# Moving the preparation items, the sums and the gate of a state-space loop by a step

## The reference

```python
xz = h @ in_proj_w.T;  x, z = split(xz, 2)
xc = silu(causal_conv4(x) + conv_b)
dt, Bm, Cm = split(xc @ x_proj_w.T);  dt = softplus(dt @ dt_proj_w.T + b)
deltaA = exp(dt[..., None] * A)                    # [B, L, 512, 16]
deltaBu = (dt * xc)[..., None] * Bm[:, :, None, :]
hst = deltaA_t * hst + deltaBu_t;  y_t = einsum('bdn,bn->bd', hst, C_t)
y = (y + D * xc) * silu(z);  out = y @ out_proj_w.T;  x = x + out
```

## Time and profile before

| | us |
|---|---|
| median of 3 runs (lowest, highest) | 2912.34 (2909.07, 2916.3) |
| the profiled execution's own time | 2912.34 |
| its span, first to last instruction | 2910.1 |
| mean granted TensorE clock | 0.89 |

### The profile page before, as it was taken

One profiled execution on the slowest core, in us unless ns is written; L12 is line 12 of the kernel. 1 busy time (PEld: TensorE's weight loads), 2 busy tenths in 40 slices (PEclk: granted clock), 3 DMA queues, 4 the chain that ended last, 5 costly groups with the idle time before them and its releaser, 6 DMA issues.

```text
span 2910.1 us, 38603 instructions
## 1 busy us (share of the span) xinstructions
PE 2412.2 (83%) x14260; PEld 1901.4 (65%) x14260; DVE 2051.3 (70%) x3042; ACT 1603.2 (55%) x2716; POOL 1052.1 (36%) x777
## 2 busy tenths in 40 slices
PE   5878787687998799858995678888777988899998
PEld 3555656566876588747883556565643443799998
DVE  6777768789997465538985767777955553567776
ACT  6665656344665455525884765656512445356663
POOL 2776767600000254210221667667811235100004
PEclk8989898889999799979997788898887787889999
DMA  4020212091000000022521220202056241246652
GB/s 150 1 95 13 83 43 76 28 358 50 23 1 1 35 1 30 12 68 91 181 82 47 94 88 8 95 1 95 12 85 108 47 103 59 86 149 218 218 207 91
DMA packets 98172, 235.14 MB, mean 81 GB/s; under 512 B 8901, under 2 KB 64977, under 8 KB 90818
## 3 DMA queue, kind: packets, MB, share of 16 engines
q1 hardware_dynamic: 85074, 209.85, 22.6%
q0 software_dynamic: 5376, 14.70, 1.5%
q10 hardware_dynamic: 7536, 8.13, 1.1%
HBM read 175.38 MB, written 48.81 MB: 77 GB/s over the span
## 4 chain that ended last, share of the span: by engine, by line
PE 51%; DVE 17%; ACT 15%; issue 7%; POOL 7%; DMA 1%; SPq 1%; POOLq 1%; ACTq 0%; DVEq 0%
PE psum L111 7%; PE psum L113 7%; PE psum L112 7%; PE psum L536 4%; PE psum L118 4%; PE psum L405 4%; PE psum L506 3%; POOL ch L430 3%; PE psum L519 2%; POOL bu L389 2%; ACT WH L3626 2%; ACT g L3773 2%; PE psum L482 2%; DVE ch L853 1%; PE psum L3067 1%
## 5 line engine op out<-in xcount | busy, mean ns | idle before, releaser
L389 POOL TENSOR_TENSOR bu<-u,row 128x1024 f32<-128x1024 f32 x158 | 371.8, 2361 | 219.8 <-DVE psum L853 132.1
L853 DVE TENSOR_TENSOR_SCAN psum<-psum,bu 128x1024 f32<-128x1024 f32 x128 | 292.7, 2287 | 94.8 <-ACT psum L663 94.8
L430 POOL TENSOR_TENSOR ch<-ch,row 128x1024 f32<-128x1024 f32 x128 | 300.8, 2355 | 149.2 <-DVE ch L853 149.2
L536 PE MATMUL psum<-ident,ch 128*128 128x128 f32 x2048 | 285.7, 288 | 69.0 <-POOL ch L430 68.3
L536 PEld LDWEIGHTS psum<-ident,ch 128*128 128x128 f32 x2048 | 247.3, 149 | 112.2 <-POOL ch L430 78.8
L853 DVE TENSOR_TENSOR_SCAN ch<-ad,psum 128x1024 f32<-128x1024 f32 x96 | 218.6, 2277 | 44.8 <-ACT ad L663 41.5
L405 PEld LDWEIGHTS psum<-row,uT 128*128 128x128 f32 x1536 | 202.7, 209 | 55.8 <-issue 36.8
L405 PE MATMUL psum<-row,uT 128*128 128x128 f32 x1536 | 208.6, 294 | 17.2 <-ACT uT L594 11.3
L663 ACT ACTIVATE psum<-dt,A 128x511 f32<-128x511 f32 x320 | 208.0, 683 | 0.3
L3773 ACT ACTIVATE g<-psum,bias 128x256 f32<-128x256 f32 x248 | 101.1, 470 | 133.8 <-PE psum L113 129.5
L875 DVE TENSOR_TENSOR ch<-psum,row 128x1024 f32<-128x1024 f32 x128 | 156.2, 1220 | 2.7
(11 more groups left out here) (469 smaller groups left out, 6954.2 us busy)
## 6 DMA issues: line engine op xcount, KB each, us to landing
W<-in_m1W SPq DMA_DIRECT2D x24, 2052.0 KB, 8.5
row<-Ascr SPq DMA_DIRECT2D x52, 512.0 KB, 4.9
row<-Bscr SPq DMA_DIRECT2D x52, 512.0 KB, 4.9
m1buf<-zt SPq DMA_DIRECT2D x8, 2048.0 KB, 16.7
W<-in_m0W SPq DMA_DIRECT2D x16, 1024.0 KB, 5.9
m1res<-ob ACTq DMA_DIRECT2D x23, 256.0 KB, 4.9
m0buf<-zt SPq DMA_DIRECT2D x2, 2064.0 KB, 17.6
xe<-m0buf SPq DMA_DIRECT2D x8, 516.0 KB, 8.1
```

Of the source, the lines that this page charges most:

```text
L389: e.tensor_tensor(m.bu[n % 2][:, :, :], u, m.row[:, g, 0, :, :], ALU.mult).then_inc(*m.fed.up)
L430: pool.tensor_tensor(o, o, m.row[:, i % UNITS, 1, :, :], ALU.mult).then_inc(*m.met.up)
L536: p = pe.matmul(m.y[:, c, :], m.ch[i % RING_C][:, j, 128 * c:128 * c + 128], k.ident, start=False, stop=g == UNITS - 1 and j == 1 and c == ...
L853: dve.tensor_tensor_scan(flat(to), flat(decays), flat(inputs), 0.0, ALU.mult, ALU.add).then_inc(*m.scan.up)
```

## The change

Three tables, two places in the order of a step, and some step numbers are changed; no computation is. On TensorE the sum of step i now follows the items of step i and the input of step i+2 (before, the input of step i+3 stood ahead of it). In `mamba_items` the items of the round before come first. The tables move most items by one step or two: z from 2-5 to 1-4, the three `yt` from 15, 19, 27 to 13, 18, 25, `out` from 7, 9, 11, 13 to 6, 8, 10, 12, `h` and `in` mostly one earlier, `conv` from 15, 16, 18, 20 to 15, 17, 19, 21, `xp` and `dt` one later. ScalarE does its part of a convolution one step after TensorE's. Its silu of z is at step 5, that of the convolution at 22, the exponentials of softplus at 26 and 27. VectorE's gate follows the first scan of the next group.

```diff
-OWN = {2: ("z", 0), 3: ("z", 1), 4: ("z", 2), 5: ("z", 3), 15: ("yt", 0), 19: ("yt", 1), 27: ("yt", 2)}
+OWN = {1: ("z", 0), 2: ("z", 1), 3: ("z", 2), 4: ("z", 3), 13: ("yt", 0), 18: ("yt", 1), 25: ("yt", 2)}
...
+    if b and s in BEFORE:
+        o.append((BEFORE[s][0], b - 1, BEFORE[s][1]))
     if s in OWN:
         o.append((OWN[s][0], b, OWN[s][1]))
...
     for i in range(PER * B):
+        s, g = i // UNITS, i % UNITS
+        for item in mamba_items(i):
+            mamba_item_pe(k, m, pe, *item)
         if i + 2 < PER * B and from_pe(i + 2):
             mamba_input_pe(k, m, pe, i + 2)
-        if i:
-            mamba_sum_pe(k, m, pe, i - 1)
-        for item in mamba_items(i):
-            mamba_item_pe(k, m, pe, *item)
-    mamba_sum_pe(k, m, pe, PER * B - 1)
+        if g == 0:
+            if s:
+                pe.wait_ge(*m.gated(s - 1))
+            pe.wait_ge(*m.dx_in(s))
...
+        pe.wait_ge(*mamba_out(m, i))
...
-        for item in mamba_items(i):
-            mamba_item_act(k, m, act, *item)
+        for item in mamba_items(i - 1) if i else []:
+            if item[0] == "conv":
+                mamba_item_act(k, m, act, *item)
+        for item in mamba_items(i):
+            if item[0] != "conv":
+                mamba_item_act(k, m, act, *item)
...
-        if n == 6:
+        if n == 5:
             mamba_gate_act(k, m, act, b)
...
-        if n == 21 and b + 1 < B:
+        if n == 22 and b + 1 < B:
             mamba_silu_act(k, m, act, b + 1)
-        if n in (25, 27) and b + 1 < B:
-            mamba_soft_exp_act(k, m, act, b + 1, n - 25, n - 23)
+        if n in (26, 27) and b + 1 < B:
+            mamba_soft_exp_act(k, m, act, b + 1, 2 * (n - 26), 2 * (n - 26) + 2)
...
-        if g == 1 and s:
+        if g == 0 and s:
             mamba_gate_dve(k, m, dve, s - 1)
```

More of the change, by code:

```diff
@@ L251 @@
 FIRST_BANKS = (0, 1, 2, 3, 4, 5, 6, 7, 0, 1, 3, 6, 2)
-OWN = {2: ("z", 0), 3: ("z", 1), 4: ("z", 2), 5: ("z", 3), 15: ("yt", 0), 19: ("yt", 1), 27: ("yt", 2)}
[L253 to L256, removed]
+OWN = {1: ("z", 0), 2: ("z", 1), 3: ("z", 2), 4: ("z", 3), 13: ("yt", 0), 18: ("yt", 1), 25: ("yt", 2)}
+BEFORE = {1: ("yt", 3), 6: ("out", 0), 8: ("out", 1), 10: ("out", 2), 12: ("out", 3)}
+AHEAD = {5: ("h", 0), 6: ("h", 1), 7: ("in", 0), 9: ("in", 1), 11: ("in", 2), 14: ("in", 3),
+         15: ("conv", 0), 17: ("conv", 1), 19: ("conv", 2), 21: ("conv", 3),
+         23: ("xp", 0), 24: ("dt", 0), 25: ("dt", 1), 26: ("dt", 2), 27: ("dt", 3), 30: ("bt", 0)}
 def mamba_items(i):
@@ L271, in mamba_items @@
         o.append((AHEAD[s][0], b + 1, AHEAD[s][1]))
-    if b and s in BEFORE:
-        o.append((BEFORE[s][0], b - 1, BEFORE[s][1]))
     return o
@@ L520, in mamba_item_pe @@
     p.then_inc(*m.full.up)
[L523 to L538, removed]
 def mamba_pe(k, m, pe):
@@ L545, in mamba_pe @@
     for i in range(PER * B):
+        s, g = i // UNITS, i % UNITS
+        for item in mamba_items(i):
+            mamba_item_pe(k, m, pe, *item)
         if i + 2 < PER * B and from_pe(i + 2):
             mamba_input_pe(k, m, pe, i + 2)
-        if i:
-            mamba_sum_pe(k, m, pe, i - 1)
-        for item in mamba_items(i):
-            mamba_item_pe(k, m, pe, *item)
-    mamba_sum_pe(k, m, pe, PER * B - 1)
+        if g == 0:
+            if s:
+                pe.wait_ge(*m.gated(s - 1))
+            pe.wait_ge(*m.dx_in(s))
+            for c in range(4):
+                p = pe.matmul(m.y[:, c, :], m.dx[:, 128 * c:128 * c + 128], k.ident, start=c == 0, stop=False, is_transpose=True)
+            p.then_inc(*m.direct.up)
+        pe.wait_ge(*mamba_out(m, i))
+        for j in range(2):
+            for c in range(4):
+                p = pe.matmul(m.y[:, c, :], m.ch[i % RING_C][:, j, 128 * c:128 * c + 128], k.ident, start=False,
+                              stop=g == UNITS - 1 and j == 1 and c == 3, is_transpose=True)
+        p.then_inc(*m.summed.up)
     mamba_item_pe(k, m, pe, "yt", B - 1, 3)
```

## The result

The changed kernel takes 2940.3 us (median of 4 runs, 2935.67 to 2942.08) against 2912.38 for the kernel before: ratio 1.0095, 95% interval 1.0077 to 1.0114. It is slower by 28 us. Forecast were 2900 us, faster by 12, with a range of 2870 to 2924: wrong in sign, and the time lies outside the range. The profiled execution took 2939.04 us, its span is 2936.8.

A forecast was written before the change was run, and what follows sets the result against it. VectorE's chain was taken as the frame, held by the order in TensorE's and ScalarE's queues. Rounds summed to −6.1 us a loop, −12.2 for two, from 2912.3 to 2900 us; range 2870 to 2924.

The forecast's parts named there:

- the start of a round: Up to scan 6 of a middle round: early gate and later inputs lose 4.7 us, bounds 0 and 6.
- the last round: Fourth round of a loop, nothing prepared for a next one: 3.7 us lost, with VectorE standing at step 24's gate.
- Steps 6 to 9: Output projection first in step 6: its large wait becomes three small ones, net loss 1.4 us including the start's.
- The wait of 9.89: VectorE's wait in us for the residual sum behind the output projection, which was held by ScalarE's silu and table load; forecast gone.
- The rival of the whole 9.89 gained: Larger gain: ScalarE catches up before step 6, 6.6 us more in four middle rounds, 2874 us; chance 0.18.
- Steps 9 to 32: Rest of a middle round: mainly an earlier x projection; step 25 is 4.1 us ahead, the round 130.9 instead of 136.3.
- the sign of a start 4 to 5 us earlier: Expected in the changed profile: the x projection starts that much earlier in the round, as u is copied before the silu.
- First round: First of a loop's four rounds: z projection ahead of the first input and later steps cost, the end gives back; 1 lost.
- Middle rounds: Second and third round of a loop: each lasts 130.9 us instead of 136.3, 5.4 saved.
- A loop: Four rounds of the state-space loop, run twice: +1.0 − 5.4 − 5.4 + 3.7 = −6.1 us.
- TensorE's lower clock as a term: At the start of a round, the sum the gate needs was taken at half clock, 1.97 us.
- The third one: Slower: gate one scan too early, its sum at half clock, 28 to 54 us, 2928 to 2954; chance 0.21.

The follow-up runs named there:

- the repeated run: The changed kernel, nothing edited, measured again on the chip of the two kernels with added zero-adding multiplications: 2937.29 us, 1.0072 of before.
- the filling: Changed kernel plus zero-adding multiplications in TensorE's idle time (9 before last sums, 3 before a round's first sum, 2 before its first z projection): 2915.94 us, 0.9996.
- 0.9913: The changed kernel with VectorE's gate back at step 1 and TensorE's old order, so new tables and late convolution copy remain: 2898.51 us.
- the mixed table: Kernel with late gate and old TensorE order, old step numbers up to 14, new from 15, items of the round before first: 2927.46 us, 1.0038.

## Why the prediction was wrong

**The step that failed.** The prediction put 4.7 us on the start of a round and priced the z projection and the input that now stand behind the first gate at full clock. Up to the scan of step 6 the start lost 5.8, 8.2 and 8.6 us in the second, third and last round. With the idle time filled, so that these multiplications do run at full clock, it lost 3.5 to 3.6 in all three. The second failed term is the last round, put at 3.7 lost and measured at 10.3.

**Start of the round: the gate right, what stands behind it too small.** 3.1 us were taken for the gate and 3.00 measured. But with 0.3 us lost, step 2 was to take 2.5 us to the next scan, and it took 4.08 in the second round and 6.66 in the third. In the third the z projection took 3.78 and the input 2.77; in the second both ran at full clock (1.98 and 1.95), and in the repeated run the z projection took 3.78 in both.

**Steps 6 to 9: right in kind.** The wait of 9.89 turned into smaller ones, 2.47 and 5.34 in the second round, where these steps took 3.1 us more than forecast. In the third the gate waited 2.57, as the 2.6 that I took, and they took 0.4 more. The rival of the whole 9.89 gained fell: ScalarE was in arrears.

**Steps 9 to 32: right, but from a later start.** From the first scan of the round, the scan of step 9 was forecast at 40.7 us and came at 44.9 and 44.7 (second and third round); step 25 at 105.1 and came at 108.5 and 110.0; the next round at 130.9 and came at 134.2 and 136.4. So most of what a middle round lacks was lost by step 9. The x projection starts 102.1 us into the round, as before, and not at 97.4; the sign of a start 4 to 5 us earlier did not come, since the lead won behind step 9 only made up for what was lost ahead of it.

**The other rounds.** First round: 1.0 lost forecast, 5.6 measured, but 0.3 in the repeated run and 4.0 and 4.1 in the second loops of the two; the x projection, 6.61 us in one first loop and 3.60 in the other, makes more than half of that difference. Middle rounds: 5.4 saved forecast, 2.1 and 0.1 measured; with the second loop and the repeated run, the mean of the middle rounds is 135.3 to 136.6 against 136.4 and 137.1 before. Last round: 3.7 lost forecast, 10.3 measured, the term most mis-sized. Its start had lost 8.1 us at step 3, where 4.7 was forecast up to step 6. The gate at step 24 waited 3.90, as forecast; the one at step 16 waited 2.29, which was put at nothing. A loop: −6.1 forecast, +13.7 measured. I had TensorE's lower clock as a term only once a round (0.9 us) and left the rest of it to a rival; filling the idle gaps took 10 to 12 of those 20 us back. The other half is not assigned to one cause.

**The rivals.** The third one, slower by an early gate at half clock, had a chance of 0.21 and 2928 to 2954 us, and 2940 lies in the middle of that. Its number came; its mechanism came only in part. It counted 0.9 to 1.8 us for each of 15 gates. In the first loop the sum that a gate waits for took 1.77 to 1.97 us at 6 of the 15, and already at 5 of them in the kernel before, where VectorE waited at most 0.43 us for it. The nine gates behind a sum at full clock hold 42.1 of the 58.9 us of gate waits; three of these stand behind x projections of 3.60 to 6.61 us, so the clock has a share there too. That the size agrees is therefore partly luck.

What the filling shows is the part that does come from the clock, and it lies mostly in the projections and inputs behind the gate. The idle time of 3.69 us ahead of the sum was not opened by the gate, since it stands in the earlier trace rows too. With the gate at step 1 and the same gap, the z projection and the input behind it take 1.98 and 1.95 us in all three rounds; with the early gate they do so in the second round only, and the z projection takes 3.78 in the other two and in all three of the repeated run. So the early gate keeps TensorE at the lower clock longer; how the three short gaps behind it (0.78, 1.15 and 0.67 us) do that is not shown.

The rule quoted from the Trainium skill ("TensorE: Matmul & The Clock Gate", Part 4: PE-mode transpose) on transposes was not tested. The drain that the Trainium skill ("ScalarE: Activation LUTs", What ACT_TABLE_LOAD costs) adds to a table load is again not in the rows: the silu starts at 286.13, where the load of 1.28 us from 284.84 ends.

What stays open: why the new order, a cost with a late gate (0.9913 to 0.9977), is a gain with an early one (1.0140 to 1.0095). The gate's waits are 74.6 against 58.9 us, with the sums in the same order to the items; that inputs come behind the sum and free TensorE for it sooner is argued, not shown.

## What to carry to other kernels

A consumer that is moved ahead of the point where its last producer can be done waits in every group: all 15 gates of the loop did, even where a large wait went elsewhere. Test such moves one by one, since here two of three parts cost 2.0 and 1.3% alone and the third gained 0.9%. When walking a new order through, price the work behind every idle gap of TensorE at both clocks, projections and inputs too, not only the first sum: after the same 3.40 us of idle time one projection took 3.60, 5.30 and 6.61 us. And look at what an item has to wait for on the other engine, not only at its place in its own queue: in the mixed table the gate behind one `yt` that stood two steps later waited 4 to 6 us in the middle rounds.

## What the runs showed that I had not expected

Filling TensorE's idle time with 9 small multiplications that add zero, 2 to 3 us of work, made the multiplications behind them run at full clock (x projection 3.60 instead of 5.15 us, sum 1.04 instead of 1.92) and a whole kernel 0.7% faster (0.9913 to 0.9847; the profiled loops 493.6 and 488.8 to 481.9 and 482.1 us). Twenty of them were too many: 6.52 us where 3.7 were idle. And the parts of the change do not add: gate and order cost 2.0% and 1.3% alone, 1.8% together with the new tables, measured from 0.9913.
